# Linear attention with pair-sorted experts: half of the second biases added by TensorE, a shorter list of loads ahead of x, routing in larger groups, a changed order at three places

## The reference

```python
xn = layernorm(x)                                    # x: [8, 256, 128], 2048 tokens
# attention: 16 heads of 8
Q, K, V = xn @ Wq, xn @ Wk, xn @ Wv
Qf, Kf = elu(Q) + 1, elu(K) + 1
Kv = einsum('bhlm,bhln->bhmn', Kf, V);  K1 = sum(Kf, axis=l)
attn = (einsum('bhlm,bhmn->bhln', Qf, Kv) / (einsum('bhlm,bhm->bhl', Qf, K1) + 1e-6)) @ Wo
# experts: E = 8, two of them for each token
vals, idx = top_k(softmax(xn @ gate_w.T + gate_b), 2)
h = relu(xn @ w1[e] + b1[e])                         # 128 -> 256
ffn = sum over the two chosen e of vals[e] * (h @ w2[e] + b2[e])
out = x + attn + ffn
```

## Time and profile before

| | us |
|---|---|
| median of 3 runs | 119.73 (119.38 to 120.27) |
| the profiled execution, its own time | 119.96 |
| span of that execution, first to last instruction | 118.2 |
| TensorE busy with matmuls, share of the span | 100.9 (85%) |
| VectorE busy | 71.0 (60%) |
| ScalarE busy | 58.4 (49%) |
| POOL busy | 50.8 (43%) |
| mean granted share of TensorE's clock | 0.962 |

### The profile page before, as it was taken

The page is one execution under the profiler, slowest core; times in us unless marked ns, Lnnn a source line. Parts: engine busy times, 40 slices in busy tenths (PEclk is TensorE's granted clock), DMA queues, the critical chain, the costliest instruction groups (busy, mean ns, idle before and its releaser), DMA issues.

```text
span 118.2 us, 3075 instructions
## 1 busy us (share of the span) xinstructions
PE 100.9 (85%) x763; PEld 91.3 (77%) x763; DVE 71.0 (60%) x291; ACT 58.4 (49%) x167; POOL 50.8 (43%) x66
## 2 busy tenths in 40 slices
PE   6967989999797897579999999999999899999100
PEld 6935968667676786469999999999999799999100
DVE  0749897998718976320575656557566565574600
ACT  1556996454020111117667676667666476666000
POOL 5004800467777778011001404022514458787870
PEclk9999999999999999967999999999999999999955
DMA  3999000002112116999855655856677758882522
GB/s 94 237 322 392 32 0 6 0 0 72 51 48 72 48 53 153 240 246 377 240 129 134 148 140 152 181 143 133 177 176 153 171 107 185 177 152 22 44 22 25
DMA packets 16656, 15.52 MB, mean 131 GB/s; under 512 B 1920, under 2 KB 16256, under 8 KB 16512
## 3 DMA queue, kind: packets, MB, share of 16 engines
q1 hardware_dynamic: 13248, 12.88, 38.8%
q0 software_dynamic: 2816, 2.18, 11.8%
q10 hardware_dynamic: 576, 0.27, 0.9%
HBM read 12.09 MB, written 3.23 MB: 130 GB/s over the span
## 4 chain that ended last, share of the span: by engine, by line
issue 28%; POOL 19%; PE 19%; DVE 13%; DMA 10%; ACT 2%; SPq 2%; POOLq 2%; DVEq 0%
POOL out L459 19%; DMA x_tok<-in_x 6%; DMA out<-res 5%; PE banks L968 4%; PE banks L937 3%; PE banks L1030 3%; PE banks L990 3%; PE banks L1005 2%; DVE att L766 2%; POOLq L115 2%; DVE rden L762 1%; SPq L354 1%; PE banks L921 1%; DVE idx L634 1%; PE banks L967 1%
## 5 line engine op out<-in xcount | busy, mean ns | idle before, releaser
L547 ACT ACTIVATE h<-banks,w_now 128x128 f32<-128x128 f32 x118 | 36.9, 364 | 19.7 <-PE banks L1061 19.7
L459 POOL DMA_INDIRECT out<-acc,token x16 | 25.0, 1562 | 34.5 <-DVE acc L795 33.3
L1061 PE MATMUL banks<-xsT,w_now 128*128 x236 | 37.5, 283 | 0.1
L1074 PE MATMUL banks<-w_all,h 128*128 x236 | 36.2, 277 | 0.3 <-DVE y L787 0.2
L1061 PEld LDWEIGHTS banks<-xsT,w_now 128*128 128x128 f32 x236 | 31.9, 197 | 0.8 <-issue 0.5
L787 DVE TENSOR_TENSOR y<-banks,w_all 128x128 f32<-128x128 f32 x59 | 17.2, 292 | 24.1 <-PE banks L1074 15.6
L1074 PEld LDWEIGHTS banks<-w_all,h 128*128 128x128 f32 x236 | 30.9, 192 | 1.0 <-issue 0.9
L795 DVE SCALAR_TENSOR_TENSOR acc<-y,xs,acc 128x128 f32 x59 | 20.7, 351 | 0.8 <-DVE y L787 0.5
L444 POOL DMA_INDIRECT sorted_dram<-xrow,slot x16 | 15.8, 990 | 5.3 <-issue 4.6
L893 PE MATMUL banks<-ones 128*128 128x128 f32 x42 | 7.9, 355 | 1.1 <-POOL ones L387 1.1
L893 PEld LDWEIGHTS banks<-ones 128*128 128x128 f32 x42 | 7.4, 265 | 1.5 <-POOL ones L387 1.1
(11 more groups left out here) (97 smaller groups left out, 108.7 us busy)
## 6 DMA issues: line engine op xcount, KB each, us to landing
w_now<-in_w1b SPq DMA_DIRECT2D x59, 129.0 KB, 2.5
w_all<-in_w SPq DMA_DIRECT2D x1, 1536.0 KB, 9.6
out<-res SPq DMA_DIRECT2D x4, 256.0 KB, 5.4
xs<-sorted_dram SPq DMA_DIRECT2D x3, 276.0 KB, 5.4
x_tok<-in_x SPq DMA_DIRECT2D x3, 256.0 KB, 6.6
xs<-sorted_dram SPq DMA_DIRECT2D x2, 138.0 KB, 3.4
x_tok<-in_x SPq DMA_DIRECT2D x2, 128.0 KB, 2.6
sorted_dram<-xrow,slot POOLq DMA_INDIRECT x16, 2.4
```

Of the source, the lines that this page charges most:

```text
L459: nc.gpsimd.indirect_dma_start(out=out_rows, out_offset=bass.IndirectOffsetOnAxis(ap=token[:, s:s + 1], axis=0), in_=acc[:, s * D:(s + 1) ...
L547: nc.scalar.activation(h[:, i % NH, c, :], h_ps[i % NHP][:, c * P:(c + 1) * P], ACT.Relu, bias=w1_now[:, i % NW, H + c:H + c + 1]).then_in ...
L1061: last = nc.tensor.matmul(h_ps[i % NHP][:, c * P:(c + 1) * P], w1_now[:, i % NW, c * P:(c + 1) * P], xsT[:, bass.ds(toff, P)], start=True, ...
L1074: last = nc.tensor.matmul(y_ps[i % NYP], h[:, i % NH, c, :], w2_all[:, bass.ds(woff + c * D, D)], start=(c == 0), stop=(c == KC - 1))
```

## The change

- Every odd visit and the last four (31 of 59) get their second bias from TensorE: a bf16 matmul of three rows (three ones by the three bf16 parts whose sum is b2) opens the bank, and the two f32 matmuls add to it. `take_y` is left out there, and `accumulate` reads the bank itself; the bank is given back by the accumulation.
- For that b2 is loaded (8 rows), split into three bf16 parts by five small POOL operations and placed on three partitions by three copies from SP.
- `wq` and the gate's bias are loaded by SP behind the constants, no longer by ScalarE's queue beside x.
- Logits are taken for four tiles at once, pairs found in groups of 8, 4 and 4 tiles, choices and the gate values of tiles 0-7 made for eight tiles at once. The banks of values and logits become four pairs of two; the first block of keys moves to another bank. `rank_rows` follows the new groups.
- VectorE: the first `finish_k` comes behind the places of the first four tiles, the second ahead of the places of the others; `divide(0)` ahead of `mask_kv(3)`; `residual(1)` ahead of `divide(3)`.
- TensorE: two instead of three filler calls behind the third transposes, and eight more filler calls ahead of the transposes of the sorted rows.

```diff
+    EARLY, LATE = slice(0, 8), slice(8, T)
+    PAIR_GROUPS = [(0, 8), (8, 12), (12, 16)]
...
-        vg_ps = [banks[:, (2, 3, 4, 6)[b % 4], 0:R * (D + E)].rearrange("p (r n) -> p r n", r=R) for b in range(B)]
-        k_ps = [banks[:, i, :].rearrange("p (t d) -> p t d", t=4) for i in (7, 1, 0, 7)]
+        vg_four = [banks[:, i:i + 2, 0:R * (D + E)].rearrange("p b (r n) -> p b r n", r=R) for i in (2, 6, 2, 6)]
+        k_ps = [banks[:, i, :].rearrange("p (t d) -> p t d", t=4) for i in (4, 1, 0, 7)]
...
+        def bias_by_pe(i):
+            return i % 2 == 1 or i >= NI - 4
+        def biases_by_dve(i):
+            return sum(not bias_by_pe(j) for j in range(i))
...
             sp.dma_start(cst[:], consts).then_inc(consts_in, 16)
+            sp.dma_start(gate_bias[:], gate_b.partition_broadcast(P)).then_inc(gate_b_in, 16)
+            sp.dma_start(wq_f[:], wq).then_inc(wq_in, 16)
             sp.dma_start(wo_f[:], wo).then_inc(wo_in, 16)
+            sp.dma_start(b2_f[:], b2).then_inc(b2_in, 16)
             sp.dma_start(w2_all[:], w2).then_inc(w2_in, 16)
+            sp.wait_ge(b2_step, 5)
+            for j in range(3):
+                sp.dma_start(b2_split[j:j + 1, :].rearrange("o (e c) -> o e c", c=WROW)[:, :, 0:D],
+                             b2_parts[j][:]).then_inc(b2_placed, 16)
...
+            def split_b2():
+                pool.wait_ge(b2_in, 16)
+                nc.gpsimd.tensor_copy(b2_parts[0][:], b2_f[:]).then_inc(b2_step, 1)
...
             fill_rows()
-            shift(0)
-            shift(1)
-            gate_values(0)
-            gate_values(1)
+            split_b2()
+            shift()
+            gate_values()
...
-            nc.scalar.dma_start(wq_f[:], wq).then_inc(wq_in, 16)
-            nc.scalar.dma_start(gate_bias[:], gate_b.partition_broadcast(P)).then_inc(gate_b_in, 16)
...
             def accumulate(i, toff, goff):
-                dve.wait_ge(y_done, i + 1)
+                if bias_by_pe(i):
+                    dve.wait_ge(l2_done, i + 1)
+                    share = y_ps[i % NYP]
+                else:
+                    dve.wait_ge(y_done, biases_by_dve(i + 1))
+                    share = y[:, i % 2, :]
...
             late_shift()
-            finish_k(0)
             pair_starts()
             places(1, slice(0, 4))
+            finish_k(0)
+            finish_k(1)
             places(2, slice(4, T))
-            finish_k(1)
...
             finish_q(2)
+            divide(0)
             mask_kv(3)
             finish_q(3)
-            divide(0)
             divide(1)
...
             keep_table()
+            residual(1)
             divide(3)
-            residual(1)
             residual(2)
...
-            def warm_up(times, after=0):
+            def warm_up(times, after=0, residuals=0):
...
+                if residuals:
+                    pe.wait_ge(res_done, residuals)
...
             def second_product(i, woff):
...
+                elif bias_by_pe(i - NYP):
+                    pe.wait_ge(acc_done, i - NYP + 1)
                 else:
-                    pe.wait_ge(y_done, i - NYP + 1)
+                    pe.wait_ge(y_done, biases_by_dve(i - NYP + 1))
+                if bias_by_pe(i):
+                    pe.wait_ge(b2_placed, 16 * 3)
+                    nc.tensor.matmul(y_ps[i % NYP], ones_bf[0:3, 0:P], b2_split[:, bass.ds(woff, D)],
+                                     start=True, stop=False)
                 for c in range(KC):
                     last = nc.tensor.matmul(y_ps[i % NYP], h[:, i % NH, c, :],
                                             w2_all[:, bass.ds(woff + c * D, D)],
-                                            start=(c == 0), stop=(c == KC - 1))
+                                            start=(c == 0 and not bias_by_pe(i)), stop=(c == KC - 1))
...
             transpose_x(2)
-            warm_up(3)
+            warm_up(2)
             project_vg(2)
+            project_vg(3)
             transpose_x(3)
-            project_vg(3)
+            project_vg(4)
             transpose_x(4)
+            project_vg(5)
             rank_rows(0)
-            project_vg(4)
-            rank_rows(1)
-            project_vg(5)
             project_vg(6)
             project_vg(7)
+            rank_rows(1)
             project_k(1)
+            project_q(0)
             rank_rows(2)
-            project_q(0)
-            rank_rows(3)
...
             pe.wait_ge(w2_in, 16)
+            warm_up(8, residuals=3)
             transpose_rows(0)
```

More of the change, by code:

```diff
@@ L129, in linear_attention_with_pair_sorted_experts @@
         wo_f = sb("wo_f", [P, D])
+        b2_f = sb("b2_f", [E, D])
+        b2_rest = sb("b2_rest", [E, D])
+        b2_parts = [sb(f"b2_part{j}", [E, D], BF16) for j in range(3)]
+        b2_split = sb("b2_split", [3, E * WROW], BF16)
         gate_bias = sb("gate_bias", [P, E])
@@ L400, in normalise, with shift @@
                                         ALU.mult).then_inc(xn_pool_done, len(NORM_POOL[i]))
[L402 to L412, removed]
+            def shift():
+                pool.wait_ge(top_done, EARLY.stop)
+                nc.gpsimd.tensor_tensor(shifted[:, EARLY, :], top8[:, EARLY, :],
+                                        top8[:, EARLY, 0:1].to_broadcast([P, 8, 8]), ALU.subtract).then_inc(shift_done, 1)
@@ L507, in copy_xT, with exp_gates @@
                 nc.scalar.copy(cols, xT_ps[i][:, 0:cols.shape[1]]).then_inc(xT_copied, 1)
[L509 to L513, removed]
+            def exp_gates(half):
+                if half == 0:
+                    act.wait_ge(shift_done, 1)
+                    nc.scalar.activation(expd[:, EARLY, :], shifted[:, EARLY, :], ACT.Exp).then_inc(exp_done, 1)
                 else:
@@ L569, in _ @@
             exp_gates(0)
-            exp_gates(1)
             exp_k(0)
-            for b in range(4, 7):
+            for b in range(4, 6):
                 copy_v(b)
             exp_k(1)
+            copy_v(6)
             copy_v(7)
             exp_q(0)
+            exp_gates(1)
             exp_k(2)
-            exp_gates(2)
             exp_q(1)
@@ L636, in find_pair @@
             def find_pair(g):
-                ts = blk_tiles(g)
+                ts = slice(*PAIR_GROUPS[g])
+                many = [P, ts.stop - ts.start, NP]
                 if g == 0:
                     dve.wait_ge(consts_in, 16)
-                dve.wait_ge(idx_done, 4 * g + 4)
+                dve.wait_ge(idx_done, ts.stop)
                 nc.vector.tensor_scalar(idxk[:, ts, :], idx8[:, ts, 0:TOP], float(BIAS_OF_KEY), None, ALU.add
@@ L872, in _ @@
                     copy_xsT(3)
-                if i == 0:
+                if i == 0 and not bias_by_pe(0):
                     take_y(0, woffs[0][0])
-                if i + 1 < NI:
+                if i + 1 < NI and not bias_by_pe(i + 1):
                     take_y(i + 1, woffs[(i + 1) // LOADS][(i + 1) % LOADS])
@@ L920, in project_vg @@
                 for r in range(R):
-                    last = nc.tensor.matmul(vg_ps[b][:, r, :], xT[:, (R * b + r) * P:(R * b + r + 1) * P],
+                    last = nc.tensor.matmul(vg_four[b // 2][:, b % 2, r, :], xT[:, (R * b + r) * P:(R * b + r + 1) * P],
                                             wkvg_f[:, D:KVG], start=True, stop=True)
@@ L949, in rank_rows @@
                 pe.wait_ge(pair_done, g + 1)
-                nc.tensor.matmul(rank_ps[:, blk_tiles(g), :], before_bf[:], of_pair[:, blk_tiles(g), :],
-                                 start=False, stop=False)
-                for t in range(4 * g, 4 * g + 4):
+                a, b = PAIR_GROUPS[g]
+                nc.tensor.matmul(rank_ps[:, a:b, :], before_bf[:], of_pair[:, a:b, :], start=False, stop=False)
+                for t in range(a, b):
                     last = nc.tensor.matmul(rank_ps[:, t + 1:T + 1, :], ones_bf[:, 0:P],
```

130 lines of the change are left out of this document (70 added, 60 removed).

## The result

The changed kernel takes **125.28 us** (median of 4 runs, 125.18 to 125.35); the kernel before, on the same chip, 119.56 (118.56 to 120.27). The ratio is 1.048, 95% interval 1.041 to 1.056: slower by nearly 5%. The profiled execution of the changed kernel took 125.35 us, its span is 123.46; that of the kernel before was 118.15.

The account below looks back on a forecast made before the run. TensorE bounds the loop over the 59 visits, almost half the span. Bias +11.0, hold-ups −0.5, tail −2.3, fillers −0.7, queue −0.4, order +0.4 sum to +7.5 us on 119.96; against the median 127.2 us, range 124.0 to 129.2.

Parts of the forecast that it names:

- the hold-ups: In the loop over the 59 visits: a slower loop covers some of TensorE's present waits, −0.5 us (0 to −1).
- the tail: Behind the last matrix start: VectorE's last accumulation and POOL's last scatter come earlier, together −2.3 us.
- the queue: Ahead of the loop: x's transfer lands earlier once query weights and gate's bias leave its queue, −0.4 us (0 to −1.1).
- the order: Ahead of the loop: larger groups, moved division and residual, ranks of eight tiles, together +0.4 us (−0.5 to +0.8).
- The price of the bias: In the loop: each of 31 bias matmuls costs TensorE 0.355 us, in all +11.0 us (1.7 to 16.1).
- The rival of the columns' price alone: In the loop: a bias matmul costs only its columns, loop +1.7 us, 119.1 us in all, not slower; chance 0.13.
- the clock: In the loop: the clock falls as the array stands still twice per odd visit, 128.8 us; chance 0.04.
- One of the signs: In odd visits of the loop: a step of about 0.8 instead of 0.447 us from second product's first start to next.
- The start: From the start of the span to the third visit: −0.7 us in all.
- Fillers: Ahead of the loop: eight filler calls hold full clock, third visit at 53.75 instead of 54.48 us, −0.7 us.
- The second residual: Ahead of the loop: moved before the last division, which then ends later than the transposes needing it start now, +0.3 us.

## Why the prediction was right

It said slower, 127.2 us, range 124.0 to 129.2; measured 125.28. The direction and its cause are shown, and four terms of the sum were mis-sized: the hold-ups (−2.1 us against the forecast), the tail (+0.7), the queue (−1.3) and the order (+0.5). These errors of 4.6 us in all cancel in part, which is luck: on the profiled executions the sum is +5.3 where it had +7.5. The direction is not luck, as the price that decides it was right.

- **The price of the bias** was taken from single-row matmuls in the attention: 0.355 us. It is 0.353, 31 times, on the path. The step that carried the forecast was the right one, and the runs with 64 and 128 rows show its mechanism. The rival of the columns' price alone does not hold even where the depth is the same (0.109 instead of 0.055), and the clock stayed at 1.00. One of the signs came out otherwise: from the start of a bias to the next product it is 0.70, not 0.8, as 0.10 of the price lies ahead of that start.
- **The hold-ups, −0.5 with a bound of −1, were −2.6**, the largest error. The prediction counted 117 products for the stretch, where 463 instructions lie in it, not quite 116 products, and so had 1.9 us of hold-ups where there are 2.5; and it took most to stay, while nothing is left (10.88 less 10.93). Most sit at one place. In the loop TensorE's sequencer loads the offsets of eight visits 14 times, 0.6 to 0.8 us each. In the kernel before, 18 starts of TensorE that are late by more than 0.02 us, 2.0 of the 2.5 us in all, come within 1.5 us behind the start of such a load; one wait of 0.3 is for first weights. With 3 and with 64 rows the loads come as often, and no start behind them is late. With 128 rows 27 late starts, 3.6 of the 4.1 us, stand there, as here, with the group of all such loads of TensorE (two lie ahead of the loop) and TensorE's weight loads in time order:

```profile
L351 PEldq TENSOR_LOAD <-table x16: 587/594/800, 45.3 to 110.0; - x16
```

```profile
67.08 0.53 PEld L1116 LDWEIGHTS banks<-w_all,h 128*128 128x128 f32 x4
67.92 0.52 PEld L1097 LDWEIGHTS banks<-xsT,w_now 128*128 128x128 f32 x4 [0.31 <-issue]
```

  One offset load lasts from 66.96 to 67.56, and the weights of the next first product, due at 67.63, load at 67.92. That the 0.35 us of each bias lets the sequencer run ahead far enough for its offset loads is how I read it. No run varies these loads, and why the 128-row bias makes the delays longer than in the kernel before (3.6 against 2.0) stays open.
- **The tail, −2.3, was −1.57.** The last accumulation ended 1.11 behind the last matrix start instead of 0.83, and accumulation 56 started at 116.08, 1.21 us behind the last start of its product (114.87): VectorE's sequencer also loads offsets, 0.76 us from 113.06 and 0.84 from 114.07, and the accumulations behind them are late. Another 0.42 of waiting ahead of accumulation 56 I can't place. POOL's last two scatters moved with it. So two accumulations, not one, start behind the last matrix start (116.66 and 117.23).
- **The start, −0.7, was −1.51**, from errors of both signs. Fillers: −0.75 from the last output product to the third visit (5.06 to 4.31), predicted −0.7. The queue: −1.68 at the last statistics, predicted −0.4 and even outside the bound of −1.1. I had shared the transfer time by bytes; 68 KB of 1,300 cost a quarter of the 6.6 us. Groups and order: +0.80 up to the first product of keys and values and +0.12 from there to the last output product, +0.92 where I had +0.4. The second residual, for which I had +0.3, lies in the 0.12. The 0.80 I put down to the copy of xT that lost its cover: I had looked at TensorE only from 16.8 us on, where it has no pause, and not at 11 to 15 us, where the new order makes one. The split between queue and order holds for this execution alone, as with the new order an earlier x is hardly passed on.

## What to carry to other kernels

Before work is moved onto the busiest engine, look for the same kind of instruction between the same neighbours in the trace and take its distance from start to start, not its columns; where the depth of a matmul differs from its neighbours', count both boundaries, as both cost here. A small load that shares the time of a transfer on the path can cost far more than its share of the bytes, so try it alone. When the tail of one engine is cut, see first which queue stands behind it.

## What the runs showed of the hardware

- A bf16 matmul of 3 or 64 rows between f32 ones of 128 rows cost TensorE 0.353 and 0.354 us, one of 128 rows 0.109, though all have 128 columns.
- A load of offsets by TensorE's sequencer takes 0.6 to 0.8 us; in the loop of the kernel before, 2.0 us of late starts stood behind 14 of them, with the bias 128 rows deep 3.6 us, with 3 or 64 rows none.
- With 68 KB in the queue beside x, the statistics of x's last part began at 10.06 to 10.31 us (three profiled executions), without them at 7.86 to 8.84 (eleven), while x's own transfers stayed the same in size: from the kernel before to the changed one the median landing of its 256 KB parts went from 6.6 to 4.6 us.
- With two more transfers of 129 KB ahead of them the five loads of the rows were issued 0.9 us later and landed 1.3 to 1.6 us later (49.57 to 54.31 us became 51.11 to 55.92).
